# Where the last stage's tensors begin, modulo 256 bytes: loaded operands at 0 and streamed ones at 64 in every projection

## The chip, the cores and the metric

The kernel runs on one core of one Trainium2 chip. The metric is the device time of one execution in microseconds. A core has TensorE (PE, matrix products; a matmul loads one operand into the array, PEld in the profile, and streams the other through it), VectorE (DVE), ScalarE (ACT), GpSimd (POOL) and SyncE (SP, which issues the transfers here). SBUF is the on-chip memory, with 128 partitions; "address" below is the byte offset inside a partition.

## The reference

An input of 2 x 4096 tokens of 256 channels goes through two residual blocks. Only the second half of the first and the second matter here; they are this kernel's last stage:

```
# per token row, after the long convolution has given yconv
y   = (yconv + xv * D_skip) * x2             # 256 channels
y   = y @ out_proj_w.T + u                   # 256 -> 256
zm  = rmsnorm(y, post_norm_w)
mlp = gelu(zm @ l1_w.T) * (zm @ l2_w.T) @ l3_w.T      # 256 -> 672 (twice) -> 256
x   = x + layernorm(y + mlp)
z   = layernorm(x)
h   = gelu(z @ (W1 + scale*m1).T + b1)       # 256 -> 1024, m1 and m2 per 512 rows rank-one terms
x   = x + layernorm(h @ (W2 + scale*m2).T + b2)       # 1024 -> 256
```

## The kernel before

The program has three phases. Phase A (to about 190 us) normalizes, projects and makes the short convolutions, phase B (to about 246 us) does the long convolution with 128-step Toeplitz matrices, phase C (`phase_c`) is everything shown above. Phase C walks over 32 units of 256 tokens (`TC = 256`) in a software pipeline: step n does the gated MLP of unit n, the second norm's turn of unit n-1, the up projection of unit n-2, the out projection of unit n+1 and the down projection of unit n-2. The first steps of each of the two batches (n = 0 to 2, 17 to 19) also make new W1 and W2 and have waits that the others have not.

Every float32 value that a product uses is split into a high and a low part in the type float32r, and a product is made of three passes: high by high, high by low, low by high. One function, `product`, issues them all: `nc.tensor.matmul(out, lhs(a, kk), rhs(b, kk))`, where `lhs` is the operand that is loaded (128 columns) and `rhs` the one that is streamed (256 columns). All those matmuls have the line of that call, 1551, in the profile, so they are told apart by tile name. In the order in which TensorE does them in a step:

| name used here | tiles in the profile | matmuls | loaded | streamed |
|---|---|---|---|---|
| MLP up | ps_ring<-mt,wl and mt,wrest | 66 | wl1, wl2, wrest | mt (called `zt` in the code) |
| turn | ps_rt<-ident,rows (L1566) | 4 | rows | ident |
| FFN up | ps_ring<-xt,we | 48 | we1 | xt |
| out | ps_o<-wout,yt | 12 | yt | wout |
| MLP down | ps_m<-wl,pt (15 per row chunk), then ps_m<-wstack,pstack (L1617) | 2 x 16 | pt, pstack | wl3, wstack |
| FFN down, chunk 0 | ps_w<-we,ht | 24 | ht | we2 |
| turn | ps_rt<-ident,rows | 4 | rows | ident |
| FFN down, chunk 1 | ps_w<-we,ht | 24 | ht | we2 |

That is 214 matmuls a step. Where TensorE would otherwise stand still near a batch's start it is given filler matmuls, `keep_running` (ps_w<-wout, L1561), which load and stream the same tile, `wout_h`.

Tensors are allocated one behind the other in SBUF in the order of the `sb(...)` calls, so an extra small tensor shifts the address of all that follow it in the same scope. Before the change one such filler, `offset` (16 floats, 64 bytes), lies in phase C between the weights and the activations.

Of the kernel before, what the change touches and what calls it, by code (L numbers as in the profile page):

```python
# [11 lines left out]
F32R = mybir.dt.float32r  # L12

P = 128
B, L, D = 2, 4096, 256
TOKENS = B * L
KB = D // P
# [9 lines left out]
H = 1024  # L27
HB = H // P
# [6 lines left out]
GROUPS = D // GC  # L35
BCONSTS = 12
SMALL = 32
FIRST = GROUPS // 2
QUAD = 4
TOEPS_EARLY = 6  # L40
TC = 256
# [34 lines left out]
def build(nc, x, pre_w, in_w, short_w, short_b, lp_chan, lp_group, lp_flat, res_chan, res_group,  # L76
          d_skip, out_w, post_w, l1_w, l2_w, l3_w, w1, b1, w2, b2, scale, out):
    x2_dram = nc.dram_tensor("x2_scratch", (P, KB, TOKENS), F32, kind="Internal").ap()
    taps_dram = nc.dram_tensor("taps_scratch", (D, 2 * CH), F32, kind="Internal").ap()
    toep_dram = nc.dram_tensor("toep_scratch", (GROUPS - TOEPS_EARLY, P, GC, CH), F32, kind="Internal").ap()  # L80
    lora_dram = nc.dram_tensor("lora_scratch", (4 * LORA, D), F32, kind="Internal").ap()
    with ExitStack() as whole:
        def sb(ctx, name, shape, dt=F32):
            return ctx.enter_context(nc.sbuf_tensor(name, shape, dt))

        def ps(ctx, name, shape):
            return ctx.enter_context(nc.psum_tensor(name, shape, F32))

        def sem(ctx, name):
            return ctx.enter_context(nc.semaphore(name))  # L90

        ident = sb(whole, "ident", [P, P])
        small = sb(whole, "small", [P, SMALL])
        neg_half = small[:, 0:2 * CA].rearrange("p (a c) -> p a c", a=2)
        neg_one = small[:, 2 * CA:2 * CA + CC]
        mark = small[:, 2 * CA + CC:2 * CA + CC + 1]
        b1s = small[:, 16:16 + HB]
        scale_s = small[:, 16 + HB:17 + HB]
        norm_scale = sb(whole, "norm_scale", [P, 2, COLS])
        norm_shift = sb(whole, "norm_shift", [P, 2, COLS])  # L100
        x2s = sb(whole, "x2s", [P, KB, TC])
        x2_in = sem(whole, "x2_in")
        y_first = [sem(whole, f"y_first{i}") for i in range(3)]
        yin = sb(whole, "yin", [P, KB, TC])


        seq = sb(whole, "seq", [P, P, KB, COLS])
        wout = [sb(whole, f"wout_{s}", [P, KB, D], F32R) for s in "hl"]
        wl1 = [sb(whole, f"wl1_{s}", [P, KB, FULL * P], F32R) for s in "hl"]
        wl2 = [sb(whole, f"wl2_{s}", [P, KB, FULL * P], F32R) for s in "hl"]  # L110

        wrest = [sb(whole, f"wrest_{s}", [P, KB, 2 * REST], F32R) for s in "hl"]
        wl3 = [sb(whole, f"wl3_{s}", [P, FULL, D], F32R) for s in "hl"]

        wstack = sb(whole, "wstack", [3 * REST, D], F32R)

        with ExitStack() as early:
            lpg = sb(early, "lpg", [P, GROUPS])
            rg = sb(early, "rg", [P, GROUPS])
            lpb_first = sb(early, "lpb_first", [P, FIRST * P])  # L120
            collect_first = sb(early, "collect_first", [P, QUAD * P])
            to_end = small[:, 17 + HB:18 + HB]
            ahead = sb(early, "ahead", [P, CH])
            own = sb(early, "own", [P, 2, KB * B, BC])
            own_high = sb(early, "own_high", [P, 2, KB * B, BC])
            later = sb(early, "later", [P, 2, KB * B, BC])
            x2_out = [sem(early, f"x2_out{i}") for i in range(2)]
            poles_in = sem(early, "poles_in")
            bconst = sem(early, "bconst")
            collect_early = sem(early, "collect_early")  # L130
            toep_early_in = sem(early, "toep_early_in")
            toep_written = sem(early, "toep_written")
            phase_a(nc, whole, sb, ps, sem, locals())
            phase_b(nc, sb, ps, sem, locals())
        phase_c(nc, sb, ps, sem, locals())


def phase_a(nc, whole, sb, ps, sem, v):
# [16 lines left out]
    with ExitStack() as ctx:  # L155
# [84 lines left out]
        def _(sp):  # L240
# [14 lines left out]
            for u in range(UA):  # L255
                if u + XBUFS + 1 < UA:
                    load_rows(u + XBUFS + 1)
                if u == 2:
                    sp.dma_start(v["lpg"][:], v["lp_group"]).then_inc(v["poles_in"], 16)
                    sp.dma_start(v["rg"][:], v["res_group"]).then_inc(v["poles_in"], 16)  # L260
                    sp.dma_start(v["lpb_first"][:], bass.AP(v["lp_flat"].tensor, 0, [[0, P], [1, FIRST * P]])
                                 ).then_inc(v["poles_in"], 16)
# [371 lines left out]
def phase_b(nc, sb, ps, sem, v):  # L634
# [13 lines left out]
    with ExitStack() as ctx:  # L648

        lpb = sb(ctx, "lpb", [P, (GROUPS - FIRST) * P])  # L650
        pole_chunk = sb(ctx, "pole_chunk", [P, GROUPS])
# [43 lines left out]
        def _(sp):  # L695
            def load(g):
                k = g - TOEPS_EARLY
                if k >= TOEPS:
                    sp.wait_ge(toep_mm, g - TOEPS + 1)
                sp.dma_start(toep[:, k % TOEPS], v["toep_dram"][k]).then_inc(toep_in[k % TOEPS], 16)  # L700

            sp.wait_ge(v["toep_written"], 16 * (GROUPS - TOEPS_EARLY))
            for g in range(TOEPS_EARLY, GROUPS):
                load(g)
                if g == FIRST - QUAD:
                    sp.dma_start(lpb[:], bass.AP(v["lp_flat"].tensor, FIRST * P, [[0, P], [1, (GROUPS - FIRST) * P]])
                                 ).then_inc(poles_more, 16)
# [86 lines left out]
        def _(act):  # L794
# [3 lines left out]
            def gather(q):  # L798

                wait(act, s_mm, q - 1)  # L800
                first = q * QUAD
                if first < FIRST:
                    poles = lpb_first[:, first * P:(first + QUAD) * P]
# [134 lines left out]
def phase_c(nc, sb, ps, sem, v):  # L938
# [6 lines left out]
    wout, wl1, wl2, wl3 = v["wout"], v["wl1"], v["wl2"], v["wl3"]  # L945
# [7 lines left out]
    PASSES_T = ((0, 0), (1, 0), (0, 1))  # L953
    ACT_HIGHS = FB - 2
    RING = 4
    OFFSET = 16
    FIRST_OUT = (14, 5, 3)
    BEFORE_TURN = {0: (8, 7, 8, 6), 2: (0, 0, 0, 6), 3: (0, 5, 0, 4), 19: (0, 5, 5, 5)}
    BEFORE_HIGH = {0: 9, 1: 10, 2: 10, 3: 9, 19: 9}
# [2 lines left out]
    HIDS = 3  # L962
    with ExitStack() as ctx:

        we1_high, we2_high = (sb(ctx, name, shape, F32R) for name, shape in
                              (("we1_h", [P, KB, H]), ("we2_h", [P, HB, D])))
        with ExitStack() as weights_made:
            base1 = sb(weights_made, "base1", [P, KB, H])
            base2 = sb(weights_made, "base2", [P, HB, D])
        we1 = [we1_high, sb(ctx, "we1_l", [P, KB, H], F32R)]  # L970
        we2 = [we2_high, sb(ctx, "we2_l", [P, HB, D], F32R)]
        b2s = sb(ctx, "b2s", [P, D])
        sb(ctx, "offset", [P, OFFSET])
        xa = sb(ctx, "xa_c", [P, CC, D])
        xb = sb(ctx, "xb_c", [P, CC, D])
        x2s = v["x2s"]
        yt = [sb(ctx, f"yt_{s}", [P, KB, TC], F32R) for s in "hl"]
        yrow = sb(ctx, "yrow", [P, 2, CC, D])
        rows = sb(ctx, "rows", [P, CC, D])
        zt = [sb(ctx, f"mt_{s}", [P, KB, TC], F32R) for s in "hl"]  # L980
        xt = [sb(ctx, f"xt_{s}", [P, KB, TC], F32R) for s in "hl"]
        gate = sb(ctx, "gate", [P, 2, TC])
        prod = sb(ctx, "prod", [P, 2, TC])
        pt = [sb(ctx, f"pt_{s}", [P, FULL, TC], F32R) for s in "hl"]

        pstack = sb(ctx, "pstack", [3 * REST, TC], F32R)
# [768 lines left out]
```

## Time and profile before

| | |
|---|---|
| median of 3 runs | 1076.98 us (1076.72 to 1077.41) |
| the profiled execution, its own time | 1076.75 us |
| span of that execution in the trace | 1075.0 us |
| TensorE busy | 1050.8 us, 98% of the span |
| VectorE, ScalarE, GpSimd busy | 82%, 66%, 28% |
| granted TensorE clock | 1.00 throughout |

The span runs from the first to the last instruction; the remaining 1.75 us of the execution lie around it. A matmul's busy time overlaps with the next one's, since they are pipelined, so the length of a run of matmuls is read from the chain of work that ended last (its rows add up to the span) or from start times, and divided by the number of matmuls.

### The profile page before, as it was taken

How to read it: one execution, taken by the hardware profiler on the slowest of the kernel's cores; microseconds unless marked ns; L12 is line 12 of the kernel's file. 1: busy time of each engine (PE TensorE's matmuls, PEld its weight loads, DVE VectorE, ACT ScalarE, POOL GpSimd, SP SyncE). 2: the span in 40 equal slices, each digit the busy share in tenths (PEclk: the TensorE clock that was granted, in tenths of full speed). 3: DMA queues.
4: the chain of work that ended last, by engine and by line, in shares of the span. 5: the costliest groups of instructions: out<-in, count | busy, mean ns of one | idle time of the engine just before them, and what ended most of it. 6: DMA issues, size and time to landing. Idle time of an engine off the chain costs nothing.

```text
span 1075.0 us, 24951 instructions
## 1 busy us (share of the span) xinstructions
PE 1050.8 (98%) x9012; PEld 1008.5 (94%) x9012; DVE 877.8 (82%) x2322; ACT 710.8 (66%) x1589; POOL 299.5 (28%) x575
## 2 busy tenths in 40 slices
PE   8899999999999999999999999999999999999998
PEld 7777888899989999999999999989999999999997
DVE  7999998774788888888887878897888888887776
ACT  7879887764456666666666666656666666666644
POOL 7677775470101112111111111111112111111111
PEclk9999999999999999999999999999999999999999
DMA  3337977986322222233222222432222223222000
GB/s 130 120 117 236 294 216 196 363 318 151 83 66 41 54 57 50 52 52 58 59 60 58 52 51 60 122 96 41 60 51 50 52 53 59 59 58 60 21 21 31
DMA packets 112491, 102.83 MB, mean 96 GB/s; under 512 B 7552, under 2 KB 103744, under 8 KB 112112
## 3 DMA queue, kind: packets, MB, share of 16 engines
q1 hardware_dynamic: 111136, 98.67, 36.2%
q0 software_dynamic: 736, 2.51, 0.6%
q8 instruction: 72, 1.18, 0.4%
q14 instruction: 51, 0.42, 0.1%
q10 hardware_dynamic: 496, 0.05, 0.0%
HBM read 75.75 MB, written 30.70 MB: 99 GB/s over the span
## 4 chain that ended last, share of the span: by engine, by line
PE 67%; DVE 6%; issue 2%; ACT 1%; POOL 0%; POOLq 0%; DVEq 0%; ACTq 0%
PE ps_ring L1551 35%; PE ps_w L1551 16%; PE ps_m L1551 9%; PE ps_o L1551 4%; PE ps_rt L1566 2%; DVE base L1373 1%; PE ps_w L1561 1%; DVE bn L1277 1%; PE ps_m L1617 1%; DVE prod L1320 0%; DVE ht_l L1289 0%; DVE pt_l L1289 0%; POOL sc L1129 0%; ACT rows L1254 0%; DVE yrow L1512 0%
## 5 line engine op out<-in xcount | busy, mean ns | idle before, releaser
L1129 POOL TENSOR_TENSOR sc<-sc,small 128x2 f32<-128x2 f32 x127 | 94.5, 744 | 676.8 <-DVE sc L1501 404.6
L1194 ACT ACTIVATE gate<-ps_ring 128x256 f32<-128x256 f32 x192 | 73.0, 381 | 129.7 <-PE ps_ring L1551 128.9
L1215 ACT ACTIVATE hid<-ps_ring,small 128x256 f32<-128x256 f32 x256 | 112.1, 483 | 24.2 <-PE ps_w L1551 13.4
L1551 PE MATMUL ps_ring<-mt_l,wl_h 128*128 128x256 f32 x640 | 125.5, 277 | 2.6 <-DVE mt_l L1289 2.6
L1551 PE MATMUL ps_ring<-mt_h,wl_h 128*128 128x256 f32 x640 | 125.5, 277 | 1.8 <-DVE prod L1320 1.3
L1551 PE MATMUL ps_ring<-mt_h,wl_l 128*128 128x256 f32 x640 | 124.9, 277 | 0.0
L1289 DVE TENSOR_TENSOR ht_l<-hid,ht_h 128x256 fp32r<-128x256 f32 x256 | 103.1, 423 | 16.5 <-ACT ht_h L1219 10.6
L1551 PE MATMUL ps_ring<-xt_h,we_h 128*128 128x256 f32 x512 | 104.8, 285 | 2.5 <-DVE prod L1320 2.4
L1551 PE MATMUL ps_ring<-xt_h,we_l 128*128 128x256 f32 x512 | 101.3, 279 | 0.0
L1551 PE MATMUL ps_ring<-xt_l,we_h 128*128 128x256 f32 x512 | 101.3, 279 | 0.0
L1320 DVE TENSOR_TENSOR prod<-ps_ring,gate 128x256 f32<-128x256 f32 x192 | 80.7, 420 | 24.2 <-ACT gate L1194 20.6
L1551 PEld LDWEIGHTS ps_ring<-mt_l,wl_h 128*128 128x128 f32 x640 | 96.5, 188 | 3.5 <-DVE mt_l L1289 3.4
L1551 PEld LDWEIGHTS ps_ring<-mt_h,wl_h 128*128 128x128 f32 x640 | 96.7, 188 | 2.6 <-DVE prod L1320 1.7
L1551 PEld LDWEIGHTS ps_ring<-mt_h,wl_l 128*128 128x128 f32 x640 | 96.5, 188 | 0.0
L507 DVE SCALAR_TENSOR_TENSOR conv<-ps_z,sw,conv 128x512 f32<-128x512 f32 x128 | 91.6, 740 | 1.9 <-ACT conv L430 1.2
L1551 PEld LDWEIGHTS ps_ring<-xt_h,we_h 128*128 128x128 f32 x512 | 77.8, 188 | 3.7 <-DVE prod L1320 3.2
L1551 PEld LDWEIGHTS ps_ring<-xt_h,we_l 128*128 128x128 f32 x512 | 78.0, 187 | 0.0
L1551 PEld LDWEIGHTS ps_ring<-xt_l,we_h 128*128 128x128 f32 x512 | 78.0, 188 | 0.0
L1173 ACT ACT_TABLE_LOAD x60 | 77.0, 1283 | 1.1
L1551 PE MATMUL ps_w<-we_h,ht_h 128*128 128x256 f32 x504 | 71.7, 284 | 0.4 <-DVE ht_h L1354 0.4
L1551 PE MATMUL ps_w<-we_h,ht_l 128*128 128x256 f32 x504 | 67.6, 276 | 0.0
L1289 DVE TENSOR_TENSOR pt_l<-prod,pt_h 128x256 fp32r<-128x256 f32 x160 | 66.7, 417 | 1.1
(203 smaller groups left out, 2720.2 us busy)
## 6 DMA issues: line engine op xcount, KB each, us to landing
toep_scratch<-taps_scratch SPq DMA_DIRECT2D x26, 512.0 KB, 7.4
toep<-toep_scratch SPq DMA_DIRECT2D x26, 512.0 KB, 8.8
xa<-in_x SPq DMA_DIRECT2D x16, 512.0 KB, 4.9
x_scratch<-x2c SPq DMA_DIRECT2D x16, 512.0 KB, 3.7
x2s<-x_scratch SPq DMA_DIRECT2D x32, 256.0 KB, 6.7
xa_c<-in_x SPq DMA_DIRECT2D x32, 256.0 KB, 2.7
xb_c<-in_x SPq DMA_DIRECT2D x32, 256.0 KB, 2.7
yin<-seq SPq DMA_DIRECT2D x124, 64.0 KB, 5.5
```

The costliest lines, as they stand in the source:

```text
L507: nc.vector.scalar_tensor_tensor(sums_of(m, u, tap), slot(b)[:], sw[:, m, tap:tap + 1], sums_of(m, u, tap), ALU.mult, ALU.add).then_inc(S[ ...
L1129: nc.gpsimd.tensor_tensor(sc[:, to], sc[:, to], neg_half[:, 0, 0:CC], ALU.pow).then_inc(S[done], 1)
L1173: nc.scalar.activation(mark_act[:], neg_half[:, 0, 0:1], function)
L1194: nc.scalar.activation(gate[rows_of, m % 2], ring[m % RING][rows_of, 0], ACT.Gelu_apprx_tanh).then_inc(S["gate_done"], 1)
L1215: nc.scalar.activation(hid[:, m % HIDS], block_of, ACT.Gelu, bias=b1s[:, m:m + 1]).then_inc(S["hid_done"], 1)
L1277: nc.vector.bn_stats(bn[:, kind, c], src[:, c]).then_inc(S[stat], 1)
L1289: nc.vector.tensor_tensor(low, src, high.bitcast(F32), ALU.subtract).then_inc(S[done], 1)
L1320: nc.vector.tensor_tensor(product_views(m)[1], value, gated, ALU.mult).then_inc(S["prod_done"], 1)
L1373: nc.vector.scalar_tensor_tensor(weights, row, col, weights, ALU.mult, ALU.add).then_inc(S["weight_add"], 1)
L1551: mm = nc.tensor.matmul(out, lhs(a, kk), rhs(b, kk), start=(j == 0), stop=(closed and j == len(todo) - 1))
L1561: nc.tensor.matmul(ps_w[:, 0], wout[0][:, 0, 0:P], wout[0][:, 0], start=True, stop=True)
L1566: mm = nc.tensor.transpose(dst[:, b, chunk(c)], src[:, c, b * P:(b + 1) * P], ident[:])
```

## The change

No instruction is added, removed or put elsewhere: engine by engine the program's rows are the same before and after but for line numbers. What changes is the order of allocations and four fillers in place of one, hence addresses.

```
+TO_STREAMED, TO_LOADED = 16, 48
...
         seq = sb(whole, "seq", [P, P, KB, COLS])
-        wout = [sb(whole, f"wout_{s}", [P, KB, D], F32R) for s in "hl"]
         wl1 = [sb(whole, f"wl1_{s}", [P, KB, FULL * P], F32R) for s in "hl"]
         wl2 = [sb(whole, f"wl2_{s}", [P, KB, FULL * P], F32R) for s in "hl"]
         wrest = [sb(whole, f"wrest_{s}", [P, KB, 2 * REST], F32R) for s in "hl"]
+        sb(whole, "to_streamed", [P, TO_STREAMED])
+        wout = [sb(whole, f"wout_{s}", [P, KB, D], F32R) for s in "hl"]
         wl3 = [sb(whole, f"wl3_{s}", [P, FULL, D], F32R) for s in "hl"]
         wstack = sb(whole, "wstack", [3 * REST, D], F32R)
...
-    OFFSET = 16
...
-        we1_high, we2_high = (sb(ctx, name, shape, F32R) for name, shape in
-                              (("we1_h", [P, KB, H]), ("we2_h", [P, HB, D])))
+        we2_high = sb(ctx, "we2_h", [P, HB, D], F32R)
+        sb(ctx, "to_loaded_c", [P, TO_LOADED])
+        we1_high = sb(ctx, "we1_h", [P, KB, H], F32R)
         with ExitStack() as weights_made:
             base1 = sb(weights_made, "base1", [P, KB, H])
+            sb(weights_made, "to_streamed_b", [P, TO_STREAMED])
             base2 = sb(weights_made, "base2", [P, HB, D])
         we1 = [we1_high, sb(ctx, "we1_l", [P, KB, H], F32R)]
+        sb(ctx, "to_streamed_c", [P, TO_STREAMED])
         we2 = [we2_high, sb(ctx, "we2_l", [P, HB, D], F32R)]
         b2s = sb(ctx, "b2s", [P, D])
-        sb(ctx, "offset", [P, OFFSET])
         xa = sb(ctx, "xa_c", [P, CC, D])
         xb = sb(ctx, "xb_c", [P, CC, D])
         x2s = v["x2s"]
-        yt = [sb(ctx, f"yt_{s}", [P, KB, TC], F32R) for s in "hl"]
...
         prod = sb(ctx, "prod", [P, 2, TC])
+
+        sb(ctx, "to_loaded_r", [P, TO_LOADED])
+        yt = [sb(ctx, f"yt_{s}", [P, KB, TC], F32R) for s in "hl"]
         pt = [sb(ctx, f"pt_{s}", [P, FULL, TC], F32R) for s in "hl"]
```

The addresses that the two built programs give, modulo 256 (high and low parts agree in each; the parts of a tensor that single matmuls read begin at multiples of 256 bytes from its start):

| block | loaded, streamed before | loaded, streamed after |
|---|---|---|
| MLP up | 0, 64 | 0, 64 |
| FFN up | 0, 64 | 0, 64 |
| out | 64, 0 | 0, 64 |
| MLP down, with wstack | 64, 0 | 0, 64 |
| FFN down | 64, 0 | 0, 64 |
| turn | 64, 128 | 64, 128 |
| filler matmuls | 0, 0 | 64, 64 |

Phases A and B are moved too. The tensors behind `to_streamed` lie 64 bytes further there, among them both operands of phase A's products; `ident` (128) and `seq` (0) stay, so the turns of phase A go from (128, 128) and (192, 128) to (192, 128) and (0, 128), and phase B's Toeplitz products stream from 192 in place of 128.

## Rows read from the trace of the kernel before

**Rows 1.** The page's first part: busy us, share, instructions of each engine

```profile
PE 1050.8 (98%) x9012; PEld 1008.5 (94%) x9012; DVE 877.8 (82%) x2322; ACT 710.8 (66%) x1589; POOL 299.5 (28%) x575
```

**Rows 2.** Busy time in windows: two whole steps

```profile
384.46:409.00 24.54, 24.54 (x216) 24.54 (x216) 19.83 (x60) 16.07 (x39) 4.23 (x8) 1.00 0.28 56
359.97:384.46 24.49, 24.49 (x216) 24.49 (x216) 19.81 (x60) 16.00 (x39) 4.24 (x8) 1.00 0.27 54
```

**Rows 3.** Chain of work, one step: start us, us, what, and number of matmuls

```profile
384.46 5.66 PE ps_ring L1551 x48
390.12 1.37 PE ps_o L1551 x12
391.49 1.70 PE ps_m L1551 x15
393.19 0.12 PE ps_m L1617
393.31 1.72 PE ps_m L1551 x15
395.02 0.12 PE ps_m L1617
395.14 2.74 PE ps_w L1551 x24
397.88 0.44 PE ps_rt L1566 x4
398.32 2.76 PE ps_w L1551 x24
401.08 7.48 PE ps_ring L1551 x66
```

**Rows 4.** Chain of work, the step that begins at 359.97 us

```profile
359.97 5.45 PE ps_ring L1551 x48
365.42 1.41 PE ps_o L1551 x12
366.83 1.77 PE ps_m L1551 x15
...
368.72 1.77 PE ps_m L1551 x15
...
370.61 2.73 PE ps_w L1551 x24
```

**Rows 5.** Chain of work, end of MLP up and FFN down, each batch's start

```profile
327.18 2.38 PE ps_ring L1551 x18
329.56 5.46 PE ps_w L1551 x48
...
729.42 2.31 PE ps_ring L1551 x18
731.73 5.66 PE ps_w L1551 x48
```

**Rows 6.** Chain of work, the last units, where MLP up has ended

```profile
1041.56 5.46 PE ps_w L1551 x48
1047.01 5.45 PE ps_ring L1551 x48
...
1058.55 4.77 PE ps_ring L1551 x42
```

**Rows 7.** TensorE in order of time: filler matmuls (start us, us, what)

```profile
319.05 1.72 PE L1561 MATMUL ps_w<-wout_h 128*128 128x256 f32 x13
```

**Rows 8.** Phase B by line: busy us, mean ns of one, idle before

```profile
L905 PE MATMUL ps_y<-toep,seq 128*64 128x128 f32 x416 | 24.2, 274 | 0.0
L919 PE MATMUL ps_y<-spread,state 64*128 64x128 f32 x256 | 16.4, 278 | 0.0
L885 PE MATMUL ps_s<-seq,collect 128*32 128x128 f32 x224 | 7.6, 276 | 0.8 <-ACT collect L807 0.8
```

More of the change, by code:

```diff
@@ L37 @@
 SMALL = 32
+TO_STREAMED, TO_LOADED = 16, 48
 FIRST = GROUPS // 2
@@ L107, in build @@
         seq = sb(whole, "seq", [P, P, KB, COLS])
-        wout = [sb(whole, f"wout_{s}", [P, KB, D], F32R) for s in "hl"]
         wl1 = [sb(whole, f"wl1_{s}", [P, KB, FULL * P], F32R) for s in "hl"]
@@ L112, in build @@
         wrest = [sb(whole, f"wrest_{s}", [P, KB, 2 * REST], F32R) for s in "hl"]
+        sb(whole, "to_streamed", [P, TO_STREAMED])
+        wout = [sb(whole, f"wout_{s}", [P, KB, D], F32R) for s in "hl"]
         wl3 = [sb(whole, f"wl3_{s}", [P, FULL, D], F32R) for s in "hl"]
@@ L955, in phase_c @@
     RING = 4
-    OFFSET = 16
     FIRST_OUT = (14, 5, 3)
@@ L963, in phase_c @@
     with ExitStack() as ctx:
-        we1_high, we2_high = (sb(ctx, name, shape, F32R) for name, shape in
-                              (("we1_h", [P, KB, H]), ("we2_h", [P, HB, D])))
+        we2_high = sb(ctx, "we2_h", [P, HB, D], F32R)
+        sb(ctx, "to_loaded_c", [P, TO_LOADED])
+        we1_high = sb(ctx, "we1_h", [P, KB, H], F32R)
         with ExitStack() as weights_made:
             base1 = sb(weights_made, "base1", [P, KB, H])
+            sb(weights_made, "to_streamed_b", [P, TO_STREAMED])
             base2 = sb(weights_made, "base2", [P, HB, D])
         we1 = [we1_high, sb(ctx, "we1_l", [P, KB, H], F32R)]
+        sb(ctx, "to_streamed_c", [P, TO_STREAMED])
         we2 = [we2_high, sb(ctx, "we2_l", [P, HB, D], F32R)]
         b2s = sb(ctx, "b2s", [P, D])
-        sb(ctx, "offset", [P, OFFSET])
         xa = sb(ctx, "xa_c", [P, CC, D])
@@ L976, in phase_c @@
         x2s = v["x2s"]
-        yt = [sb(ctx, f"yt_{s}", [P, KB, TC], F32R) for s in "hl"]
         yrow = sb(ctx, "yrow", [P, 2, CC, D])
@@ L983, in phase_c @@
         prod = sb(ctx, "prod", [P, 2, TC])
+        sb(ctx, "to_loaded_r", [P, TO_LOADED])
+        yt = [sb(ctx, f"yt_{s}", [P, KB, TC], F32R) for s in "hl"]
         pt = [sb(ctx, f"pt_{s}", [P, FULL, TC], F32R) for s in "hl"]
```

## The prediction

> **What bounds the kernel now.** I read the page's first part first: TensorE is busy 98% of the span, the next engine 82% [rows 1]. Then one step of the last stage in a window: TensorE busy in 24.54 of 24.54 us, VectorE in 19.8, ScalarE in 16.1, at full granted clock [rows 2]. So in a step nothing is waited for, and its length is that of its 214 matmuls, ten pieces and one more turn in the chain [rows 3]. 26 of the 32 MLP up blocks of the chain are rows like the last of that group (7.48 us, 66 matmuls), so 26 steps are of this kind.
>
> Dividing pieces by their matmuls gives the second fact. MLP up takes 7.48 / 66 = 113.3 ns for a matmul, FFN up 5.66 / 48 = 117.9 ns [rows 3], although both load from 0 and stream from 64, in the same shapes. The same FFN up took 5.45 us, 113.5 ns, in one of the steps [rows 4]; of the 27 FFN up blocks without a wait that follow a turn, 25 took 5.66 and two took 5.45. FFN down (load 64, stream 0) shows both paces too: 5.46 us for 48 in one batch, 5.66 in the other [rows 5]. So there are two paces, about 113.4 and 117.9 ns, each pair of addresses has been seen at both, and a block keeps the pace with which it starts, over 48 and 66 matmuls. A third one is that of the fillers, whose load and stream begin at the same address: (1.72 - 0.28) / 12 = 120 ns, 0.28 being the last matmul's own length [rows 7].
>
> What picks the pace? In the rows it depends on what stands before:
> - behind a turn, (load 0, stream 64) runs slow in 25 of 27 blocks, and (64, 0) runs fast in every step: FFN down's second half is 2.76 us for 24, which is 2.72 and a start some 40 ns dearer [rows 3];
> - where (0, 64) changes to (64, 0) without a turn, the pace swaps: slow FFN up, then out at 1.37 us for 12 (114 ns) [rows 3]; fast FFN up, then out at 1.41 (118) and MLP down at 1.77 for 15 (118) [rows 4]; the end of MLP up in 2.38 us, then FFN down fast; the same end in 2.31, then FFN down slow [rows 5] (0.07 over some 16 matmuls is again 4.4 ns for each);
> - but from fast (64, 0) to (0, 64) it stays fast: FFN down, then MLP up at 113.3 ns [rows 3], and FFN down 5.46, then FFN up 5.45 near the end [rows 6].
>
> MLP up, the largest block, owes its fast pace to the last of these: it is handed over by a fast FFN down with the other pair of addresses.
>
> **The change, part by part.** No instruction moves and none is added. Turns, MLP up and FFN up keep their addresses modulo 256. Out, MLP down and FFN down, blocks of 12, 32, 24 and 24 matmuls, go from (load 64, stream 0) to (0, 64), the pair of MLP up and FFN up.
>
> (1) FFN up behind its turn: same addresses as before, so I leave it at 5.66 us. (2) Out and MLP down follow it with the same addresses now, so no change of sides swaps the pace; they stay slow, as MLP up and FFN up do over whole blocks. Out 1.37 to 1.41, MLP down 1.70 to 1.77 and 1.72 to 1.77, the lengths that they have when slow [rows 4]: 0.04 + 0.07 + 0.05 = 0.16 us. The two stack matmuls load 96 rows and could disturb the pace; when slow, MLP down stayed slow behind the first of them [rows 4], so I add nothing. (3) FFN down, chunk 0: 24 x 117.9 = 2.83 in place of 2.74, 0.09. (4) FFN down, chunk 1, now has the situation of FFN up, (0, 64) behind a turn, which is slow in 25 of 27: 2.83 in place of 2.76, 0.07. (5) MLP up follows at the same addresses, keeps the slow pace: 66 x 117.9 = 7.78 in place of 7.48, 0.30. The sum is 0.62 us in a step of 24.54, and 26 steps give 16.1 us. Nothing hides it, since TensorE waits for nothing there.
>
> (6) Outside those steps: at the end FFN down and FFN up go from 5.46 and 5.45 to 5.66, the last FFN up from 4.77 to 42 x 117.9 = 4.95 [rows 6], the last MLP down adds 0.12: 0.7. At the first batch's start FFN down goes from 5.46 to 5.66 (at the second's it is slow already) [rows 5], with an out and MLP down beside it: 0.3. The two steps whose FFN up was fast lose 0.21 there but have slow out and MLP down already: 0.1 for both. Together 1.1. (7) Fillers keep equal addresses on both sides, at 120 ns [rows 7], and cover waits: nothing. (8) Phase A's products have both operands moved alike, nothing. Its turns are four matmuls at a time; the last stage's, with 64 and 128, take 0.44 us for four [rows 3], and I take 0. Phase B's 416 Toeplitz matmuls take 24.2 us, 58 ns each, for 128 streamed columns [rows 8]. Half of the difference between paces (256 columns, 4.5 ns), 2.3 ns for each, would be 1 us; I take 0 and keep 1 us for the range, to either side.
>
> The profiled execution's span is 1075.0 us, its time 1076.75. 1075.0 + 16.1 + 1.1 = 1092.2, and 1.75 around it give 1093.95; the median of the runs is 0.23 above the profiled one, so 1094.
>
> **The rivals.** *All fast.* The mechanism: with one pair of addresses in all projections there is no change of sides left that upsets the pace, and the hand-over from one step to the next settles at the fast pace, as two steps did [rows 4]. What decides is the first block behind each turn: if both start fast, all stays fast. Then FFN up loses 0.22, out 0.01, MLP down 0.02, FFN down 0.02 + 0.04: 0.31 a step, 8.1 in 26, with 0.4 at the batches' starts 1068.5 us. For it: the start behind a turn depends on the timing of what stands ahead, and that changes everywhere; equal pace is also what the two fast steps show. Against it: 25 of 27.
>
> *Partly slow.* Still the slow pace, but not everywhere. One turn leads to the slow pace, the other to the fast, or a stack matmul turns slow into fast. Slow from FFN up to chunk 0 and fast behind: 0.16 + 0.09 - 0.04 = 0.21 a step, 1082.5. The other way round: -0.27 + 0.07 + 0.30 = 0.10 a step, 1079.6. Slow, broken by the first stack matmul until the turn: 0.62 less 0.05 and 0.11 and 0.02, 0.44 a step, 1088.4.
>
> *No change.* The paces have nothing to do with addresses, only with the timing at a block's start, and the same program falls into them as before: 1077. The trace has both paces at the same addresses [rows 3, 4], which speaks for it; that the swap comes with each change of sides, in both batches [rows 5], and the fillers' 120 ns speak against it.
>
> The Trainium skill, "SBUF — State Buffer", section "Who interferes with whom", says that PE has two independent read ports, one for the streamed operand and one for LDWEIGHTS, and that "PE and ACT never wait on anyone"; by that rule a move of addresses is worth nothing and the time stays at 1077. The trace fits that rule badly: its fillers and its two paces have the same engine, clock and shapes and different lengths.
>
> **How the numbers follow.** All slow 0.42 (1094, its own range 1091 to 1097), partly slow 0.26 (1079.5 to 1090), no change 0.10, all fast 0.22 (1066 to 1072.5, with mixtures up to 1074.8). A measurement of this kernel tells 0.2%, 2.2 us, from no change, so slower is 0.68, same 0.10, faster 0.22. The range has to hold 8 in 10: 1072 to 1097 leaves out most of all fast and little above.
>
> **What would show it.** In the chain of the changed kernel, per step: MLP up 7.78 in place of 7.48 is the main sign; out 1.41, MLP down 1.77 and 1.77, FFN down 2.83 and 2.83, FFN up still 5.66; a step of 25.16 us. Fast rows (FFN up 5.45) in most steps prove the first rival. I am wrong if the first block behind a turn starts fast, or if pace is not handed from block to block at equal addresses.

## The result, and the profile after

The changed kernel takes 1088.49 us (median of 4 runs, 1086.44 to 1090.5). The kernel before, run beside it, takes 1076.85 us. The ratio is 1.0112 [1.0094, 1.013], so the change makes the kernel 1.1% slower: 11.6 us, where 17 were forecast. The profiled execution took 1089.49 us, with a span of 1087.8 us, 12.8 more than before.

First the page's engine row for TensorE of the changed kernel, which answers to [rows 1].

```profile
PE 1063.4 (98%) x9012; PEld 1022.0 (94%) x9012; DVE 880.5 (81%) x2322; ACT 711.4 (65%) x1589; POOL 298.9 (27%) x575
```

The same number of instructions keeps TensorE busy 12.6 us longer. That is nearly the whole difference of the spans, so time has gone into the matmuls and not into waits. Next the windows view of three whole steps of the changed kernel, with the columns of [rows 2].

```profile
511.67:536.82 25.15, 25.15 (x216) 25.15 (x216) 19.88 (x60) 16.11 (x39) 4.26 (x8) 1.00 0.27 54
536.82:561.58 24.76, 24.76 (x216) 24.76 (x216) 19.79 (x60) 16.05 (x38) 4.23 (x8) 1.00 0.26 54
561.58:586.40 24.82, 24.82 (x216) 24.82 (x216) 19.88 (x60) 16.06 (x40) 4.25 (x8) 1.00 0.27 55
```

TensorE is still never idle and the granted clock is still full. The other engines do the same work in the same time. But the step is longer, and it has three lengths that take turns. The forecast had one, 25.16 us. Now the chain of work of the changed kernel: an all slow step, then the end of the second step and most of the third (start us, us, what).

```profile
511.67 5.65 PE ps_ring L1556 x48
517.32 1.41 PE ps_o L1556 x12
518.74 1.77 PE ps_m L1556 x15
...
520.62 1.77 PE ps_m L1556 x15
...
522.51 2.83 PE ps_w L1556 x24
...
525.78 2.83 PE ps_w L1556 x24
528.61 7.77 PE ps_ring L1556 x66
...
550.93 2.73 PE ps_w L1556 x24
553.66 7.48 PE ps_ring L1556 x66
...
561.58 5.45 PE ps_ring L1556 x48
567.02 1.36 PE ps_o L1556 x12
568.38 1.70 PE ps_m L1556 x15
570.08 0.12 PE ps_m L1622
570.20 1.77 PE ps_m L1556 x15
...
572.09 2.83 PE ps_w L1556 x24
```

Read the lengths against [rows 3] and [rows 4]. The first step is the forecast, row for row: 5.65, 1.41, 1.77, 1.77, 2.83, 2.83, 7.77. In the second, FFN down chunk 1 comes out of the turn at the fast pace (2.73), hands it to MLP up (7.48), and FFN up is fast behind the next turn too (5.45), then out (1.36) and MLP down chunk 0 (1.70). The stack matmul at 570.08 ends the fast stretch: the next 15 matmuls take 1.77.

In the whole chain, MLP up is slow in 18 of 26 blocks and fast in 8 (before: fast in 26). FFN down chunk 1 is slow in 18 of 26. FFN up is fast in 9 of 28 (before: 3 of 28). In all 9 steps that start fast, the fast stretch ends at the first stack matmul. Three steps take 74.73 us where three of 24.54 took 73.62, so a step costs 0.37 us more, 9.6 in 26. Of the 11.05 us by which the last stage has grown, from its first filler to its last matmul, 1.4 lie outside those steps.

The rest of the 12.8, 1.7 us, lies ahead of the last stage. Its first filler starts at 248.35 us where it started at 246.65. That start varies from one profile to another: in the fourteen profiles of this study it lay between 245.86 and 248.50. Two kernels with the changed kernel's addresses in phases A and B had it at 245.86 and 246.21, and one with the addresses of before (experiment 9) at 248.31. So I read the 1.7 as scatter.

### The profile page after: what moved, and what is told of

It reads as the page before. It is cut to its first block, busy times and chain, and to the rows that moved or that the text cites. A ratio compares the mean times of both kernels' runs of the same rounds, so it can differ in the third digit from the quotient of the medians.

```text
span 1087.8 us, 24951 instructions
## 1 busy us (share of the span) xinstructions
PE 1063.4 (98%) x9012; PEld 1022.0 (94%) x9012; DVE 880.5 (81%) x2322; ACT 711.4 (65%) x1589; POOL 298.9 (27%) x575
## 4 chain that ended last, share of the span: by engine, by line
PE 68%; DVE 6%; issue 2%; ACT 1%; POOL 0%; POOLq 0%; DVEq 0%; ACTq 0%
PE ps_ring L1556 36%; PE ps_w L1556 16%; PE ps_m L1556 9%; PE ps_o L1556 4%; PE ps_rt L1571 2%; DVE base L1378 1%; PE ps_w L1566 1%; DVE bn L1282 1%; PE ps_m L1622 1%; DVE prod L1325 0%; DVE ht_l L1294 0%; POOL sc L1134 0%; ACT rows L1259 0%; DVE pt_l L1294 0%; DVE x L1525 0%
## 5 line engine op out<-in xcount | busy, mean ns | idle before, releaser
L1556 PE MATMUL ps_w<-we_l,ht_h 128*128 128x256 f32 x504 | 69.2, 279 | 0.0
```

The lines of the kernel that those rows point to most:

```text
L1556: mm = nc.tensor.matmul(out, lhs(a, kk), rhs(b, kk), start=(j == 0), stop=(closed and j == len(todo) - 1))
```

## The experiments

All of them are variants of the allocation, or of what stands between blocks, and the median of the kernel before stands beside each. "(64, 0)" is again loaded at 64, streamed at 0, modulo 256 bytes.

**1. FFN up alone at (64, 0), the rest as before.** Three fillers, the two high weights in the other order, and `xt` allocated ahead of `offset`.

```diff
+        we2_high = sb(ctx, "we2_h", [P, HB, D], F32R)
+        sb(ctx, "to_64", [P, 16])
+        we1_high = sb(ctx, "we1_h", [P, KB, H], F32R)
...
+            sb(weights_made, "to_0_b", [P, 48])
             base2 = sb(weights_made, "base2", [P, HB, D])
...
+        sb(ctx, "to_0", [P, 48])
         we2 = [we2_high, sb(ctx, "we2_l", [P, HB, D], F32R)]
...
+        xt = [sb(ctx, f"xt_{s}", [P, KB, TC], F32R) for s in "hl"]
         sb(ctx, "offset", [P, OFFSET])
```

> The kernel before, with only FFN up turned round: we1 begins at 64 modulo 256 (loaded), xt at 0 (streamed); all other pairs as before. Theory (a block's pace is handed on at equal addresses, and (load 64, stream 0) behind a turn runs fast): FFN up goes from 5.66 to about 5.49 us (48 x 113.4 and a start some 40 ns dearer), out stays 1.36 to 1.37, MLP up stays 7.48; 0.18 us a step, some 5 us in all, about 1072. Rival 1 (FFN up is slow for another reason than its addresses, such as ScalarE and VectorE writing beside it): FFN up stays at 5.66, about 1077. Rival 2 (any change only shuffles the timing): MLP up is slow in some steps, 1077 to 1088.

Measured: 1071.57 us (8 runs, 1070.55 to 1075.76) against 1076.67; ratio 0.9958 [0.9946, 0.997]. It is, with experiment 8, the fastest kernel of this study. Chain of work of this kernel, one step:

```profile
505.60 5.46 PE ps_ring L1554 x48
511.06 1.36 PE ps_o L1554 x12
512.42 1.70 PE ps_m L1554 x15
...
516.07 2.74 PE ps_w L1554 x24
...
519.24 2.76 PE ps_w L1554 x24
522.01 7.48 PE ps_ring L1554 x66
```

Every block of this step is fast. The changed starting addresses of two tensors moved FFN up from 5.66 to 5.46 and out from 1.37 to 1.36, and the other lengths stayed. FFN up was slow in 25 of 28 blocks and is slow in one now: 24 times 0.21 is 5.0 us, measured 5.1. That the starting addresses of its operands set the pace of a block is hereby shown in the direction that gains; that it is their value modulo 256 that counts follows with experiment 4.

**2. The changed kernel, with FFN down back at (64, 0).** The last block ahead of MLP up has its old addresses again; out and MLP down keep the new ones. The last filler stands ahead of `ht`.

```diff
+        sb(ctx, "to_loaded_c", [P, TO_LOADED])
         we2_high = sb(ctx, "we2_h", [P, HB, D], F32R)
-        sb(ctx, "to_loaded_c", [P, TO_LOADED])
...
-            sb(weights_made, "to_streamed_b", [P, TO_STREAMED])
...
-        sb(ctx, "to_streamed_c", [P, TO_STREAMED])
...
+        sb(ctx, "to_streamed_c", [P, TO_STREAMED])
         xa = sb(ctx, "xa_c", [P, CC, D])
...
+        sb(ctx, "to_64", [P, 16])
```

> The changed kernel, with only FFN down turned back: ht at 64 (loaded), we2 at 0 (streamed), as before; out and MLP down stay at (0, 64). Theory: FFN down's first half is fast again (slow (0, 64) swaps to fast (64, 0)), the second half fast behind its turn, MLP up 7.48 in every step by hand-over; out and MLP down stay slow behind a slow FFN up (0.16 us a step): about 1077 + 4 = 1081. Rival (the paces come from timing alone, and addresses only shift it): MLP up stays at 7.77 in two of three steps, about 1088.

Measured: 1083.44 us (1082.13 to 1085.49) against 1076.67; ratio 1.007 [1.0054, 1.0087]. Chain of work of this kernel:

```profile
513.46 1.41 PE ps_o L1556 x12
514.87 1.77 PE ps_m L1556 x15
...
518.64 2.83 PE ps_w L1556 x24
521.48 0.44 PE ps_rt L1571 x4
521.91 2.76 PE ps_w L1556 x24
524.68 7.48 PE ps_ring L1556 x66
```

MLP up is fast again in 25 of 26, behind FFN down chunk 1, fast in 25 of 26; the one slow MLP up stands behind the one slow chunk 1. So step (5) of the prediction holds: MLP up has the pace of the block ahead of it. But chunk 0, which comes behind slow blocks at (0, 64), is at (64, 0) itself and should have swapped to fast, stayed slow in 22 of 26. That is 0.09 a step and 2 us in all, most of the difference to the 1081 expected. Between it and MLP down stands a stack matmul. My rule of the swap doesn't hold there.

**3. The changed kernel with stack matmuls of 128 rows.** `pstack` and `wstack` get 32 more rows of zeros, written once by VectorE, and TensorE waits once for that; the products are the same.

```diff
-        wstack = sb(whole, "wstack", [3 * REST, D], F32R)
+        wstack = sb(whole, "wstack", [P, D], F32R)
...
-        pstack = sb(ctx, "pstack", [3 * REST, TC], F32R)
+        pstack = sb(ctx, "pstack", [P, TC], F32R)
...
+            for t in (pstack, wstack):
+                nc.vector.memset(t[3 * REST:, :].bitcast(F32), 0.0).then_inc(S["stack_zero"], 1)
...
+                if n == 0:
+                    pe.wait_ge(S["stack_zero"], 2)
```

> The changed kernel, with the stack matmul (96 rows) padded to 128 rows: pstack and wstack get 32 rows of zeros, set once, addresses as in the changed kernel. Theory A (its 96 rows are what turns the fast pace into the slow one in every step where MLP down starts fast): a fast block stays fast through MLP down and FFN down's first half; if the turn keeps it, every step after the first fast one is fast, 24.2 us a step, down to 1069; if the turn breaks it in one of several, in between, 1072 to 1084. Theory B (it is the other tensor, whatever its rows): nothing changes, 1088.

Measured: 1092.29 us (1092.12 to 1093.7) against 1076.67; ratio 1.0149 [1.0134, 1.0164]. Chain of work of this kernel, its first step, the one in which FFN up started fast:

```profile
335.14 5.45 PE ps_ring L1559 x48
...
343.64 0.11 PE ps_m L1627
343.76 1.70 PE ps_m L1559 x15
...
345.57 2.73 PE ps_w L1559 x24
348.30 0.44 PE ps_rt L1574 x4
348.73 2.83 PE ps_w L1559 x24
351.56 7.78 PE ps_ring L1559 x66
```

Two findings. In the one step that starts fast, the fast pace now passes through both stack matmuls up to the turn (2.73), which it did in 0 of 9 cases with 96 rows. And all 26 MLP up blocks are slow: this kernel is the one that the prediction described, and it costs 15.6 us, near the 17.2 forecast. So whether a third of the steps starts fast depends on the rows of the stack matmuls, though a turn stands between them and the block that starts fast. By what it depends on them this run does not show.

**4. The changed kernel's order of allocation, with the addresses of before.** The four fillers are left out and one of 64 bytes is put where `offset` was.

```diff
-        sb(whole, "to_streamed", [P, TO_STREAMED])
-        sb(ctx, "to_loaded_c", [P, TO_LOADED])
-            sb(weights_made, "to_streamed_b", [P, TO_STREAMED])
-        sb(ctx, "to_streamed_c", [P, TO_STREAMED])
+        sb(ctx, "offset", [P, TO_STREAMED])
         xa = sb(ctx, "xa_c", [P, CC, D])
...
-        sb(ctx, "to_loaded_r", [P, TO_LOADED])
```

> The changed kernel's order of allocations with the residues modulo 256 of the kernel before: fillers taken out but for 64 bytes in front of xa, so that wout, wl1, wl2, wl3, we1, we2 and the activations lie at other addresses than before but at the same ones modulo 256. Theory (only the residues matter): 1077 within 0.2%, with the same pattern of slow FFN up and fast MLP up. Rival (it is the whole address, or any move): it differs from 1077 by more than 2 us.

Measured: 1076.77 us (10 runs) against 1076.67; ratio 1.0004 [0.9995, 1.0013]. The blocks have the pattern of before, but for one slow MLP up of 26. The order of the tensors and their whole addresses are worth nothing that could be measured; the addresses modulo 256 make the difference.

**5 to 7. One pair of addresses in all projections: (64, 0), (0, 128), (0, 0).** In these three, `mt`, `xt` and `rows` (at 64 as ever) are also allocated ahead of `xa`. The edit of the first; the other two have other sizes in the same places or no filler there, and one more filler behind `rows`.

```diff
+        sb(whole, "pad_wl", [P, 16])
...
-        sb(whole, "to_streamed", [P, TO_STREAMED])
+        sb(whole, "pad_ws", [P, 48])
...
-        sb(ctx, "to_loaded_c", [P, TO_LOADED])
+        sb(ctx, "pad_c1", [P, 16])
...
-            sb(weights_made, "to_streamed_b", [P, TO_STREAMED])
+            sb(weights_made, "pad_b", [P, 48])
...
-        sb(ctx, "to_streamed_c", [P, TO_STREAMED])
+        sb(ctx, "pad_c2", [P, 48])
...
+        zt = [sb(ctx, f"mt_{s}", [P, KB, TC], F32R) for s in "hl"]
+        xt = [sb(ctx, f"xt_{s}", [P, KB, TC], F32R) for s in "hl"]
+        sb(ctx, "pad_r", [P, 16])
+        rows = sb(ctx, "rows", [P, CC, D])
```

> Every projection at (load 64, stream 0), MLP up and FFN up too; rows stay at 64 for the turns. Theory (what the changed kernel lost is not that all pairs are equal, but which pair it is: (64, 0) starts fast behind a turn, and a stack matmul disturbs it for some 20 ns only): every block fast, as in the first experiment, 1071 to 1073. Rival (equal pairs everywhere are what lets the slow pace run on, either way round): MLP up slow in many steps, 1080 to 1090.

> Every projection at (load 0, stream 128); rows stay at 64. A pair that no run had so far in these shapes. If only the equality of residues costs (120 ns against 113 to 118), a pace of 113.3 or 117.8 as with 64: 1069 to 1094. If the two sides run over each other's residues in a matmul whatever the start, it is between these and 120: up to 1106.

> Every projection loads from 0 and streams from 0; rows stay at 64. Theory (equal residues cost 120 ns for a matmul, as in the fillers): 206 projections a step x 120 ns = 24.7 us and two turns of some 0.46 us, 25.6 us a step in place of 24.54, some 29 us in 27 steps: 1106. Rival (addresses have no price in themselves, and the fillers are slow for writing and reading one tile over and over): 1077 to 1094.

Measured, against 1076.87 us: (64, 0) 1079.35, ratio 1.0026 [1.0012, 1.004]; (0, 128) 1098.55, ratio 1.0204 [1.0189, 1.0219]; (0, 0) 1106.87, ratio 1.0279 [1.0263, 1.0294]. Chain of work of the kernel with all at (64, 0):

```profile
507.15 5.66 PE ps_ring L1556 x48
512.81 1.41 PE ps_o L1556 x12
...
521.17 2.74 PE ps_w L1556 x24
523.91 7.49 PE ps_ring L1556 x66
```

The same view of the kernel with all at (0, 128):

```profile
505.04 7.82 PE ps_ring L1556 x66
...
513.30 5.69 PE ps_ring L1556 x48
```

The same view of the kernel with all at (0, 0):

```profile
508.44 7.89 PE ps_ring L1552 x66
...
516.77 5.75 PE ps_ring L1552 x48
```

At (0, 0) a matmul of FFN up takes 5.75 / 48 = 119.8 ns in all 28 blocks, the pace of the fillers [rows 7], and one of MLP up 7.89 / 66 = 119.5; the kernel costs 30 us more than before. So the fillers are not slow for loading and streaming one tile over and over. At (0, 128) a matmul takes 118.5 ns in each of the two (5.69 / 48, 7.82 / 66). Of the three distances tried, only 64 bytes between the two sides gave two paces and a memory of which one is on. The (64, 0) kernel breaks the theory that I had by then, that (64, 0) always starts fast behind a turn, and its rival too, since MLP up stayed fast in 26 of 26. What became slow is FFN up, with out and MLP down behind it. FFN up at (64, 0) was fast in 27 of 28 blocks in experiment 1, where MLP up ahead of the turn is at (0, 64). Here, with MLP up at (64, 0), it was slow in 25 of 28. So how a block starts depends on what stood ahead of the turn as well.

**8. Experiment 1 with stack matmuls of 128 rows.** The edits of 1 and 3 together.

> The first experiment's kernel (FFN up at (64, 0), all else as before), with the stack matmul padded to 128 rows of zeros as in the third. Theory: the disturbance of about 20 ns behind each of the two stack matmuls goes, 0.04 us a step, 1.1 us in all: 1070.5. Rival (the stack matmul also sets the phase with which the turn is entered, as the third experiment showed for the changed kernel): FFN down or FFN up starts slow behind a turn in some steps, 1072 to 1085.

Measured: 1072.87 us (1071.62 to 1074.06) against 1076.87; ratio 0.9962 [0.9949, 0.9975]. FFN down chunk 0 went from 2.74 to 2.72 and MLP down chunk 1 from 1.72 to 1.70, so the 20 ns that a stack matmul costs the block behind it are gone. But MLP up was slow twice and FFN up twice, in the second full step of each batch. It is no better than experiment 1, as the rival had it.

**9 and 10. One transpose more in a turn, no address touched.** In 9 the kernel before repeats its first transpose in the turn ahead of FFN up. In 10 the changed kernel repeats it in the turn between the halves of FFN down. The repeated transpose writes the same values to the same place. The edit of 10; that of 9 is the same at the call that increments `xt_mm`.

```diff
-            def transpose_unit(dst, src):
+            def transpose_unit(dst, src, extra=0):
+                for _ in range(extra):
+                    nc.tensor.transpose(dst[:, 0, chunk(0)], src[:, 0, 0:P], ident[:])
...
-                transpose_unit(ps_t, rows).then_inc(S["zt_mm"], 1)
+                transpose_unit(ps_t, rows, 1).then_inc(S["zt_mm"], 1)
```

> The kernel before, no address touched, with one more transpose (a repeat of the first) in the turn ahead of FFN up, five in place of four. It costs 0.11 us a step, 3.5 us in 32. Theory (the pace behind a turn is set by the phase in which it is entered and left, addresses only decide which phases hold): FFN up starts fast in some or all steps (5.45 to 5.49 in place of 5.66); if in all, 1077 + 3.5 - 5.5 = 1075, and out and MLP down may turn slow behind it (0.16 a step, 1079). Rival (what decides is the pair of addresses alone): FFN up stays 5.66 in 25 of 27, 1080.5.

> The changed kernel, no address touched, with one more transpose in the turn between FFN down's halves. It costs 0.11 us a step, 3.5 us in 32. Theory (phase): the regular pattern of one fast step in three changes, to always slow (1088.5 + 3.5 + 5.5 = 1097), always fast behind this turn (1080 to 1084) or another mixture. Rival (addresses alone): one in three as before, 1092.

Measured: 9 took 1081.01 us (10 runs, 1079.73 to 1083.11) against 1077.47, ratio 1.0028 [1.0013, 1.0043]. FFN up was slow behind all 27 turns, where the theory expected fast starts. The price is the transpose itself, some 0.11 us a step, and the two fast steps of before, which are gone. 10 took 1088.6 us against 1077.47, ratio 1.0098 [1.0064, 1.0131]. Chain of work of 10:

```profile
524.33 0.11 PE ps_rt L1570
524.44 0.44 PE ps_rt L1573 x4
524.88 2.73 PE ps_w L1556 x24
...
549.42 2.83 PE ps_w L1556 x24
552.25 7.77 PE ps_ring L1556 x66
```

With five transposes ahead of it, FFN down chunk 1 is fast in 13 of 26 steps and not in 8, and MLP up likewise: every second step in place of every third. The extra 0.11 us a step and the additional fast blocks cancel in the time. That one transpose more shifts the share of fast steps, with no address touched, is shown; which length of a turn gives which start is not.

**11. The changed kernel with `rows` at 0.** The turns then load from 0 in place of 64, and all else keeps its address modulo 256.

```diff
+        sb(ctx, "rows_to_0", [P, 48])
         rows = sb(ctx, "rows", [P, CC, D])
+        sb(ctx, "rows_to_64", [P, 16])
```

> The changed kernel with rows, which the turns load, at 0 in place of 64 (ident, which they stream, stays at 128); all else at the same residues. The turns' own length (0.44 us for four) should stay, as phase A's turns are as long at other residues. Theory (the phase on leaving a turn comes from TensorE's last loads and streams, the turn's pair included): another share of fast steps than one in three, anywhere from 1074 to 1094. Rival (the turn's residues don't matter): one in three, 1088.

Measured: 1094.61 us (1093.34 to 1097.04) against 1077.47; ratio 1.0155 [1.0124, 1.0186]. The turns still take 0.44 us for four, but all 26 MLP up blocks and all 28 FFN up blocks are slow. Where one operand of four transposes begins decides the pace of the 66 matmuls that come a block later.

**12. The kernel before with FFN down alone at (0, 64).** The part of the change that stands ahead of MLP up, by itself.

```diff
-        we1_high, we2_high = (sb(ctx, name, shape, F32R) for name, shape in
-                              (("we1_h", [P, KB, H]), ("we2_h", [P, HB, D])))
+        we1_high = sb(ctx, "we1_h", [P, KB, H], F32R)
+        sb(ctx, "to_64", [P, 16])
+        we2_high = sb(ctx, "we2_h", [P, HB, D], F32R)
+        sb(ctx, "to_0", [P, 48])
...
+            sb(weights_made, "to_64_b", [P, 16])
...
+        sb(ctx, "to_64_c", [P, 16])
...
-        sb(ctx, "offset", [P, OFFSET])
...
+        sb(ctx, "to_0_h", [P, 48])
```

> The kernel before with the other part of the change alone: FFN down goes to (load 0, stream 64), while out and MLP down stay at (64, 0). Theory (the large loss is that MLP up is handed its pace by an FFN down that has its own pair of addresses and starts slow behind the turn): FFN down's second half 2.83 and MLP up 7.77 in most steps, out and MLP down fast as before (1.37, 1.70): 0.37 us in each such step, up to 10 us, 1082 to 1087. Rival (only all pairs together make the slow pace run on): MLP up stays 7.48, 1077.

Measured: 1092.54 us (1091.02 to 1093.4) against 1077.23; ratio 1.0144 [1.0127, 1.0161]. Chain of work of this kernel:

```profile
510.74 5.65 PE ps_ring L1554 x48
516.39 1.41 PE ps_o L1554 x12
...
521.58 2.83 PE ps_w L1554 x24
...
524.85 2.83 PE ps_w L1554 x24
527.68 7.77 PE ps_ring L1554 x66
...
535.89 5.66 PE ps_ring L1554 x48
541.54 1.37 PE ps_o L1554 x12
```

MLP up is slow in 26 of 26. FFN down's addresses alone bring the whole loss and 4 us more than the whole change does, and putting FFN down back alone (experiment 2) recovers MLP up. I had expected 1082 to 1087: chunk 0 was slow too, and out and MLP down, whose addresses were those of before, were slow in 15 of 27 steps. The rows show more: slow FFN up at (0, 64) hands on to out at (64, 0) with nothing between them, and out is slow in one step (1.41) and fast in the next (1.37). My rule of the swap held behind 11 of 24 slow FFN up blocks in this kernel, where it held behind all 24 in the kernel before.

## Why the prediction was right, and where its size was off

The direction was right, and so was the hand-over of the slow pace from FFN down to MLP up, which is the largest term. The start behind a turn was right in two steps of three only, and the prediction itself had named a fast start there as the sign that it is wrong. The likeliest case, all slow, was too dark: 11.6 us measured, 17 forecast. 1088.5 lies below that case's own range (1091 to 1097) and in that of *partly slow* (1079.5 to 1090), which had a chance of 0.26. The stated range of 1072 to 1097 holds *no change* as well, so that the time fell into it says little by itself.

- **(1) FFN up stays slow.** Right in 19 of 28. In 9 it started fast: 8 times behind a fast MLP up, and once in the first batch's first full step, behind slow blocks. A fast MLP up ahead is not the reason by itself, since in the kernel before it stood ahead of the slow FFN up blocks too.
- **(2) Out and MLP down slow, 0.16 a step, "the two stack matmuls ... I add nothing".** The lengths were right in the slow steps (1.41, 1.77, 1.77). The second half was wrong. I had looked at one slow step, where the pace stayed slow behind the stack matmul. A fast one turns slow there, 9 times of 9, and with 128 rows (experiment 3) it did not in the one case there was. In that kernel, where all 26 MLP up blocks were slow, the forecast came within 1.7 us (1092.3 for 1094).
- **(3) Chunk 0 slow, 0.09.** Right in 26 of 26.
- **(4) Chunk 1 slow behind its turn.** The step that was mis-sized: I took the 25 of 27 of FFN up for it, and it was 18 of 26. Equal addresses behind a turn do not make an equal start.
- **(5) MLP up takes over the pace ahead of it, 0.30.** Right in each of the 26 blocks; experiments 2 and 12 show it from both sides. With 18 slow ones in place of 26 the term is 5.3 us in place of 7.8. Together with FFN up, out and half of MLP down, which are fast in a third of the steps, 16.1 became 9.6.
- **(6) Outside the steps 1.1.** Measured 1.4. **(7), (8)** Fillers still 1.72 us for 13, phase B's 416 Toeplitz matmuls still 24.2 us.

Of the rivals, *all fast* fell for this pair of addresses, though a kernel that is fast in nearly all blocks exists: not with one pair everywhere, but with FFN up at (64, 0) between blocks at (0, 64) and (64, 0). *Partly slow* is the nearest description of what happened. Its third variant gave 1088.4, the measured time, but for a wrong reason: it had the stack matmul turn slow into fast, and it turns fast into slow. *No change* fell with experiments 1 and 7, and experiment 4 shows that the same addresses modulo 256 give the same time again. The same instructions with the same data took 1071.6, 1076.8 and 1106.9 us by addresses alone. So the rule of the Trainium skill, "SBUF — State Buffer", section "Who interferes with whom", that PE's streamed operand and weight load have independent ports and that PE never waits on anyone, does not give the time of this kernel; whether the two sides share a port or something behind the ports no run shows. What TensorE loses shows in no wait of the profile, only in the length of its blocks.

What stays open: how the start of a block behind a turn is decided. It depends on the block's pair of addresses (FFN up before against 1), on the pair ahead of the turn (1 against 5), on the turn's own addresses (11), on its length (10) and on the rows of the stack matmuls (3). The chain shows one more thing, that two fast blocks need not be alike. Chunk 1 of FFN down takes 2.76 us in most steps of the kernel before and 2.74 in two. This is one of the two, and the FFN up that follows behind the next turn is the fast one of [rows 4], at 359.97:

```profile
349.31 2.74 PE ps_w L1551 x24
352.05 7.49 PE ps_ring L1551 x66
```

In the kernels with MLP up and FFN up both at (0, 64), FFN up behind MLP up started fast in all 26 cases in which chunk 1 had taken 2.73 or 2.74, and slow in all others, 92 with 2.76 and 107 with 2.83. With FFN up at (64, 0) and MLP up at (0, 64) (1, 8) it is the other way round: slow in the 3 cases with 2.74, fast in the 47 others. So some 20 ns in one block go together with the start of a block 66 matmuls and a turn later. With both at (64, 0) (5) this doesn't hold, and what lies behind it I can't say.

The swap at a change of sides is no rule either. It held between FFN up and out in the kernel before, failed there in half of the steps of experiment 12, and behind a stack matmul in 2; and in 12 the fast (64, 0) of MLP down did not stay fast in chunk 0 at (0, 64), where a stack matmul stands between them. Neither pace needs a transfer beside it: in the last FFN up block (42 matmuls, 4.77 us before and 4.96 after) the DMA share is 0.00 in both kernels. VectorE and ScalarE are not excluded. They read and write the tensors that were moved, and they are busy beside TensorE at either pace, so whether its two sides alone get in each other's way is not shown. Steps finer than 64 bytes weren't tried.

## What to carry to other kernels

Where TensorE is busy all the time, divide the length of each block of matmuls by their number and compare blocks of equal shape; a difference of 4% or 6% at full clock, with no wait, can come from where the loaded and the streamed operand begin modulo 256 bytes. In this kernel 64 bytes between the two were cheaper than 128 or 0. Try the pairs on the whole kernel, because a block inherits its pace from the one ahead, and what a layout gives can't be told from one block. Here the best was not the uniform layout but the one in experiment 1, 0.42% faster than before and some 1.5% faster than the change (0.9958 / 1.0112).

## What the runs showed of the hardware

- Four paces of one and the same matmul (float32r, 128 columns loaded, 256 streamed, full granted clock, 2.4 GHz): 113.3 ns (7.48 us for 66, which is 272 periods) and 117.8 ns (7.77 for 66, 283 periods) with 64 bytes between the sides, 118.5 ns (7.82 for 66) with 128 bytes, 119.5 to 120 ns (7.89 for 66, and the fillers) with equal addresses modulo 256.
- The two paces at 64 bytes are sticky: a block of up to 66 matmuls keeps the one with which it starts, and at equal addresses a block directly behind it takes it over. At (0, 64) one matmul that loads 96 rows turned the fast pace into the slow one in 24 of 24 cases (the changed kernel, experiments 2 and 10). At (64, 0) it cost the block behind it 20 ns and the pace stayed fast (25 of 25 in the kernel before).
- The transposes of a turn took 0.44 us for four with their sides at (64, 128) and at (0, 128) alike, but the choice decided the pace of what followed: 18 of 26 MLP up blocks slow with the one, 26 of 26 with the other.
